# Reordering the start of a perceiver layer: the first pair of x loaded and normalised alone, a fold in two blocks, a query between scores, and ranks in two fp32r matmuls

## The reference

```python
x = x + xattn(layernorm(x), ctx)      # softmax((x Wq + bq)(ctx Wk + bk)^T / 16) (ctx Wv + bv) Wo + bo
x = x + attn(layernorm(x))            # causal, one head of 256
h = layernorm(x)
raw = h @ centroids.T                 # 8 experts
top_idx = top_k(sigmoid(raw + routing_bias), 2)
x = x + shared(h) + sum over the 2 chosen experts of gate * (gelu(h @ Wfc_e) @ Wproj_e)   # width 1024
```

## Time and profile before

| | |
|---|---|
| median of 3 timed runs | 253.61 us (253.21 to 254.71) |
| profiled execution, its own time | 252.07 us |
| its span, first to last instruction | 250.3 us |
| outside the span | 1.77 us |
| TensorE matmul busy | 97% of the span |
| VectorE, ScalarE, GpSimd busy | 61%, 55%, 20% |
| mean rate of all transfers | 296 GB/s |

### The profile page before, as it was taken

How to read it: one execution, slowest core, us unless ns; L and a number is a source line. 1 busy time by engine, 2 the same in 40 slices (tenths; PEclk the granted TensorE clock), 3 DMA queues, 4 the chain that set the end, 5 groups by cost and what they waited for, 6 DMA issues and landing times.

```text
span 250.3 us, 5122 instructions
## 1 busy us (share of the span) xinstructions
PE 242.9 (97%) x1908; PEld 209.6 (84%) x1908; DVE 152.4 (61%) x365; ACT 137.2 (55%) x271; POOL 50.6 (20%) x81
## 2 busy tenths in 40 slices
PE   7999999999999999999998999999999999999994
PEld 6857646366467599999998899999999999999994
DVE  1722246545635788788759147666766766667683
ACT  0725206052152688796776166666666666666641
POOL 5100000000100010420686002102122222226700
PEclk9999999999999999999999999999999999999999
DMA  7999999999999999930166358999989999920132
GB/s 249 425 432 402 417 415 427 384 405 429 351 376 385 352 347 429 427 143 0 67 187 261 101 152 283 373 356 369 370 346 358 363 360 364 335 107 21 56 135 84
DMA packets 13870, 74.12 MB, mean 296 GB/s; under 512 B 1524, under 2 KB 8444, under 8 KB 9500
## 3 DMA queue, kind: packets, MB, share of 16 engines
q1 hardware_dynamic: 12700, 70.59, 74.4%
q0 software_dynamic: 1008, 2.76, 2.9%
q10 hardware_dynamic: 144, 0.53, 0.6%
HBM read 67.56 MB, written 6.32 MB: 295 GB/s over the span
## 4 chain that ended last, share of the span: by engine, by line
PE 72%; DMA 15%; POOL 3%; DVE 3%; ACT 3%; issue 2%; SPq 1%; POOLq 0%; DVEq 0%; ACTq 0%
PE psum L512 64%; DMA raw<-experts_dram 9%; PE psum L760 4%; POOL slot_x_dram L479 3%; DMA slot_x_dram<-second,rows_of 3%; DMA squares<-squares_dram 2%; PE psum L601 1%; PE psum L778 1%; DMA xrow<-slot_x_dram 1%; ACT prob L885 1%; PE psum L821 1%; DVE xn L1046 1%; PE psum L552 0%; PE psum L650 0%; PE psum L692 0%
## 5 line engine op out<-in xcount | busy, mean ns | idle before, releaser
L512 PE MATMUL psum<-xrowT,ring 128*128 128x128 f32 x480 | 58.3, 275 | 0.0
L512 PEld LDWEIGHTS psum<-xrowT,ring 128*128 128x128 f32 x480 | 56.2, 192 | 0.0
L1301 DVE TENSOR_TENSOR dlo<-ring,dhi 128x1024 fp32r<-128x1024 f32 x30 | 38.4, 1281 | 3.7 <-ACT dhi L968 3.7
L1320 DVE TENSOR_TENSOR slot_hlo<-slot_h,slot_hhi 128x512 fp32r<-128x512 f32 x30 | 20.8, 692 | 30.0 <-ACT slot_hhi L996 30.0
L994 ACT ACTIVATE slot_h<-psum 128x512 f32<-128x512 f32 x30 | 18.0, 600 | 35.7 <-PE psum L512 35.7
L512 PE MATMUL psum<-dhi,slot_hhi 128*128 128x256 f32 x120 | 36.3, 302 | 0.1
L512 PE MATMUL psum<-dhi,slot_hlo 128*128 128x256 f32 x120 | 33.8, 282 | 0.0
L512 PE MATMUL psum<-dlo,slot_hhi 128*128 128x256 f32 x120 | 33.8, 282 | 0.0
L968 ACT ACTIVATE dhi<-ring 128x1024 fp32r<-128x1024 f32 x30 | 31.1, 1040 | 0.0
L504 POOL DMA_INDIRECT results_dram<-y_rows,result_row x13 | 15.6, 1199 | 71.8 <-DMA results_dram<-y_rows,result_row 55.3
L512 PE MATMUL psum<-xh,parted 128*128 128x256 f32 x128 | 26.8, 286 | 0.1
(11 more groups left out here) (195 smaller groups left out, 408.2 us busy)
## 6 DMA issues: line engine op xcount, KB each, us to landing
ring<-experts_dram SPq DMA_DIRECT2D x15, 2048.0 KB, 8.2
ctx<-ctx_dram SPq DMA_DIRECT2D x4, 3072.0 KB, 24.5
ctxT_start<-ctxT_start_dram SPq DMA_DIRECT2D x4, 2048.0 KB, 19.0
ctxT_rest<-ctxT_rest_dram SPq DMA_DIRECT2D x4, 1154.0 KB, 21.8
raw<-experts_dram SPq DMA_DIRECT2D x2, 2048.0 KB, 16.4
slot_x_dram<-empty_row SPq DMA_DIRECT2D x1, 1935.0 KB, 16.9
xrow<-slot_x_dram SPq DMA_DIRECT2D x15, 129.0 KB, 7.1
squares<-squares_dram SPq DMA_DIRECT2D x1, 1285.0 KB, 14.2
```

Source lines behind the costliest of these rows:

```text
L512: return pe.matmul(out, lhsT, rhs, start=first, stop=last)
L1301: dve.tensor_tensor(dlo[b % 2][:, steps, :], ring[b][:, steps, C * P:STEP_W], dhi[b % 2][:, steps, :].bitcast(F32), ALU.subtract).then_inc ...
L1320: dve.tensor_tensor(slot_hlo[:, half, :], slot_h[:, half, :], slot_hhi[:, half, :].bitcast(F32), ALU.subtract).then_inc(slot_hlo_ready, 1)
```

## The change

Transfers: pair 0 of x is loaded alone, then squares 0 and 1 in two pieces (one for each half k of the contraction, 1028 contiguous bytes each), then pairs 1 to 3 of x, all on SyncE's queue. cols goes to ScalarE's queue.

Start: VectorE computes the statistics of pair 0 and normalises it before it waits for the rest of x. GpSimd computes rstd of pair 0 between two of its constants, the others after all of them. TensorE folds k = 0 for both halves of the output when its piece is there, then k = 1; transposes and queries pair 0 alone, then pairs 1 and 2 together, and pair 3's query stands between score chunks 1 and 2. ScalarE loads its table early with a copy of one element, copies pair 0 before the broadcasts, and makes two of the three broadcasts later. vecs gets its own bank (2) and is made before wrow.

Ranks: chosen, before, tri and a second matrix of ones are fp32r. before gets a fifth column group in place of total, and ranks are two matmuls, of 40 and 32 columns.

```diff
@@ -118,7 +118,8 @@
         neghalf = sb("neghalf", [P, T])
-        tri = sb("tri", [P, P])
+        tri = sb("tri", [P, P], F32R)
+        ones_r = sb("ones_r", [P, P], F32R)
         ones = sb("ones", [P, P])
@@ -147,6 +148,7 @@
         lsum2 = sb("lsum2", [P, 2])
+        first_of_table = sb("first_of_table", [P, 1])
@@ -155,9 +157,8 @@
         gat = sb("gat", [P, TOP, T, ROUTED])
-        chosen = sb("chosen", [P, T, ROUTED])
-        before = sb("before", [P, T, ROUTED])
-        total = sb("total", [P, ROUTED])
+        chosen = sb("chosen", [P, T, ROUTED], F32R)
+        before = sb("before", [P, T + 1, ROUTED], F32R)
         rank = sb("rank", [P, T, ROUTED])
@@ -259,8 +260,10 @@
-        x_in, query_squares_in, squares_in, cols_in, rows_in = (
-            sem("x_in"), sem("query_squares_in"), sem("squares_in"), sem("cols_in"), sem("rows_in"))
+        x_start_in, x_rest_in, squares_in, cols_in, rows_in = (
+            sem("x_start_in"), sem("x_rest_in"), sem("squares_in"), sem("cols_in"), sem("rows_in"))
+        query_squares_in = [sem("query_squares0_in"), sem("query_squares1_in")]
+        vec_ps, vecs_ready = sem("vec_ps"), sem("vecs_ready")
         ctx_in, ctx_rest_in = [sem("ctx0_in"), sem("ctx1_in")], [sem("ctx0_rest_in"), sem("ctx1_rest_in")]
@@ -314,7 +317,7 @@
-        NORMS = {item: 2 + n for n, item in enumerate(item for item in ORDER if item[0] in ("proj", "z"))}
+        NORMS = {item: 3 + n for n, item in enumerate(item for item in ORDER if item[0] in ("proj", "z"))}
@@ -327,8 +330,10 @@
         def _(sp):
-            sp.dma_start(xs[:, :, :], x_d).then_inc(x_in, 16)
-            sp.dma_start(cols[:, :, :], cols_d.rearrange("(c p) n -> p c n", p=P)).then_inc(cols_in, 16)
+            sp.dma_start(xs[:, 0:1, :], x_d[:, 0:1]).then_inc(x_start_in, 16)
+            for c in range(C):
+                sp.dma_start(squares[:, 0:2, c, :], squares_d[:, 0:2, c, :]).then_inc(query_squares_in[c], 16)
+            sp.dma_start(xs[:, 1:T, :], x_d[:, 1:T]).then_inc(x_rest_in, 16)
@@ -430,13 +435,15 @@
             pool.wait_ge(consts, 4)
-            link(pool.memset(tri[:, :], 1.0))
-            pool.affine_select(out=tri[:, :], in_=tri[:, :], compare_op=ALU.is_ge, fill=0.0, base=-1,
+            pool.tensor_copy(ones_r[:, :], ones[:, :])
+            pool.affine_select(out=tri[:, :], in_=ones[:, :], compare_op=ALU.is_ge, fill=0.0, base=-1,
                                pattern=[[1, P]], channel_multiplier=-1).then_inc(consts, 1)
...
             pool.wait_ge(consts, 6)
+            pool.wait_ge(var_ready, 1)
+            pool.tensor_tensor(rstd[:, 0:1], veps[:, 0:1], neghalf[:, 0:1], ALU.pow).then_inc(rstd_ready, 1)
             link(pool.iota(iota128[:, :], pattern=[[P, ROUTED]], base=0, channel_multiplier=0,
@@ -446,14 +453,14 @@
                            allow_small_or_imprecise_dtypes=True))
-            link(pool.memset(before[:, 0, :], 0.0))
+            link(pool.tensor_copy(before[:, 0, :], empty_row[:, 0:ROUTED]))
             link(pool.memset(ones8[:, :], 1.0))
...
             pool.wait_ge(consts, 7)
-            pool.wait_ge(var_ready, 1)
-            pool.tensor_tensor(rstd[:, :], veps[:, :], neghalf[:, :], ALU.pow).then_inc(rstd_ready, 1)
+            pool.wait_ge(var_ready, 2)
+            pool.tensor_tensor(rstd[:, 1:T], veps[:, 1:T], neghalf[:, 1:T], ALU.pow).then_inc(rstd_ready, 1)
             for what, *args in ORDER:
@@ -511,14 +518,6 @@
-            def fold(b, left, right):
-                for m in range(C):
-                    for k in range(C):
-                        ins = mm(bank(b, m * D, D), squares[:, left, k, m * P:(m + 1) * P],
-                                 squares[:, right, k, 0:D], k == 0, k == C - 1)
-                ins.then_inc(fold_ps, 1)
             def fold_vec(b, at, left, col):
@@ -538,37 +537,50 @@
-            pe.wait_ge(query_squares_in, 16)
-            fold(0, XWQT, XWKT)
+            for k in range(C):
+                pe.wait_ge(query_squares_in[k], 16)
+                for m in range(C):
+                    ins = pe.matmul(bank(0, m * D, D), squares[:, XWQT, k, m * P:(m + 1) * P], squares[:, XWKT, k, 0:D],
+                                    start=k == 0 and m == 0, stop=k == C - 1, skip_group_check=True)
+            ins.then_inc(fold_ps, 1)
+            def transpose_x(t, b, at):
+                pe.wait_ge(xn1_ready, t + 1)
+                for c in range(C):
+                    ins = pe.transpose(bank(b, at + c * P, P), xn[:, t, c * P:(c + 1) * P], ident[:, :])
+                return ins
+            def query(t, b, at):
+                for m in range(C):
+                    for k in range(C):
+                        ins = mm(bank(b, at + m * P, P), aq[:, k, m * P:(m + 1) * P],
+                                 xT[:, k, t * P:(t + 1) * P], k == 0, k == C - 1)
+                return ins
+            pe.wait_ge(consts, 2)
+            transpose_x(0, PT, 0).then_inc(xT_ps, 1)
             pe.wait_ge(cols_in, 16)
-            fold_vec(1, D + 1, XWKT, XBQ)
+            fold_vec(2, 0, XWKT, XBQ).then_inc(vec_ps, 1)
             pe.wait_ge(bcast_ready, 1)
             fold_row(1, 0, XWQT).then_inc(fold_ps, 1)
-            pe.wait_ge(consts, 7)
-            for t in range(T):
-                pe.wait_ge(xn1_ready, t + 1)
-                for c in range(C):
-                    ins = pe.transpose(bank(PT + t // 2, (t % 2) * D + c * P, P),
-                                       xn[:, t, c * P:(c + 1) * P], ident[:, :])
-                if t % 2 == 1:
-                    ins.then_inc(xT_ps, 1)
             pe.wait_ge(fold_act, 1)
-            for t in range(T):
-                pe.wait_ge(xT_sb, t // 2 + 1)
-                tok = slice(t * P, (t + 1) * P)
-                for m in range(C):
-                    for k in range(C):
-                        ins = mm(bank(PO + t // 2, (t % 2) * D + m * P, P), aq[:, k, m * P:(m + 1) * P],
-                                 xT[:, k, tok], k == 0, k == C - 1)
-                if t % 2 == 1:
-                    ins.then_inc(q_ps, 1)
+            pe.wait_ge(xT_sb, 1)
+            query(0, PO, 0).then_inc(q_ps, 1)
+            transpose_x(1, PT + 1, 0)
+            transpose_x(2, PT + 1, D).then_inc(xT_ps, 1)
+            transpose_x(3, CHAIN, 0).then_inc(xT_ps, 1)
+            pe.wait_ge(xT_sb, 2)
+            query(1, PT, 0)
+            query(2, PT, D).then_inc(q_ps, 1)
+            def last_query():
+                pe.wait_ge(xT_sb, 3)
+                query(3, CHAIN, 0).then_inc(q_ps, 1)
             def scores(t, ch):
-                if t % 2 == 0 and ch == 0:
-                    pe.wait_ge(q_sb, t // 2 + 1)
-                if t == 0 and ch == 0:
-                    pe.wait_ge(fold_act, 1)
+                if ch == 0:
+                    pe.wait_ge(q_sb, (1, 2, 2, 3)[t])
+                if t == 0 and ch == 1:
                     pe.wait_ge(fold_dve, 1)
@@ -692,10 +704,14 @@
-            for ch in range(SCH):
+            for ch in range(2):
                 scores(0, ch)
+            last_query()
+            for ch in range(2, SCH):
+                scores(0, ch)
             pe.wait_ge(squares_in, 16)
+            pe.wait_ge(q_sb, 2)
             for m in range(C):
@@ -706,7 +722,6 @@
             ins.then_inc(fold_ps, 1)
-            pe.wait_ge(q_sb, 2)
             pe.wait_ge(bcast_ready, 2)
@@ -714,6 +729,7 @@
             def bias_folds():
+                pe.wait_ge(q_sb, 3)
                 fold_vec(CHAIN, D + 1, AWK, ABQ)
@@ -729,11 +745,10 @@
                 pe.wait_ge(chosen_ready, 1)
+                mm(bank(RANK_BANK, 0, (T + 1) * ROUTED), ones_r[:, :], before[:, :, :].rearrange("p t e -> p (t e)"),
+                   True, False)
                 mm(bank(RANK_BANK, 0, T * ROUTED), tri[:, :], chosen[:, :, :].rearrange("p t e -> p (t e)"),
-                   True, False)
-                mm(bank(RANK_BANK, 0, T * ROUTED), ones[:, :], before[:, :, :].rearrange("p t e -> p (t e)"),
-                   False, True)
-                mm(bank(RANK_BANK, T * ROUTED, ROUTED), ones[:, :], total[:, :], True, True).then_inc(rank_ps, 1)
+                   False, True).then_inc(rank_ps, 1)
@@ -855,30 +870,46 @@
-            act.dma_start(squares[:, 0:2], squares_d[:, 0:2]).then_inc(query_squares_in, 16)
-            act.wait_ge(consts, 7)
-            act.wait_ge(cols_in, 16)
-            for n, col in enumerate((XBK, XBV, ABK)):
+            act.dma_start(cols[:, :, :], cols_d.rearrange("(c p) n -> p c n", p=P)).then_inc(cols_in, 16)
+            act.wait_ge(warm_ready, 1)
+            act.activation(first_of_table[:, :], sm[:, 0:1], ACT.Copy)
+            def spread(n, col):
                 for c in range(C):
...
+            def xT_copy(n, start, stop, b):
+                act.wait_ge(xT_ps, n + 1)
+                act.activation(xT[:, :, start * P:stop * P].rearrange("p c (t n) -> p t c n", n=P),
```

(72 more changed lines are left out.)

## The result

The changed kernel took 255.89 us as a median of 8 runs (254.50 to 256.75), the kernel before 254.04 us beside it (253.21 to 254.99). The ratio is 1.0077, with a 95% interval of 1.0050 to 1.0105: slower by 0.8%. The prediction, 253.5 us with a range of 252.3 to 254.6, was wrong in its time and on the wrong side. The ratios are taken over the fast runs alone, which leaves out 3 of the 11 runs of e5 and 5 of the 12 of e14; medians and ranges are of all runs.

The account below looks back on a forecast made before the run. Up to 84 us the full transfer stream, beside a full TensorE, was taken to set the landings. 0 (start) + 0.1 (stream) - 0.2 (ranks) = -0.1 us on 253.61 gave a median of 253.5 us, range 252.3 to 254.6.

Parts of the forecast that it names:

- the new wait for ctxT_start 1: Sign: TensorE newly waits for this transfer at about 30.5 us; with ctx's wait at 50.7, as long as the start's gain.
- Ranks: Two single-pass matmuls replace three two-pass ones; the scatter starts 0.2 us earlier (0 to 0.4), and this reaches the end.
- Start on TensorE: Up to the second matrix's fold at 20.43 us: 0.7 us gained (-0.8 to +1.5), worth 0 at the end.
- a cap: Landings at 30.5, 50.7 and 81.9 us are set by the stream, limiting an earlier start's gain to TensorE's slack there.
- R3: Rival: the start's small steps make TensorE 0.8 us late at the second fold; 253.9 us, chance 10%.
- Stream: Same bytes, moved by three terms; +0.1 us at raw 0 and at 83.94 us, bounds -0.4 and +1.2.
- Term (a): Squares 0 and 1 and pair 0 of x in pieces of about 1 KB, at 356 against 418 GB/s: +0.3 us.
- (c): Slow first 6 us: cols' small rows now travel beside pair 0, filling idle engine time; -0.4 to 0, taken as -0.2.
- Term (b): SyncE issues ctxT_start 0 behind five transfers, some 0.9 us later; costs up to 0.9 us, taken as 0.
- R2: Rival: engines run dry between 1.6 and 4 us, landings move by 0.9 and 0.3 us; 254.6 us, chance 10%.
- R4: Rival: pair 0 of x doesn't land earlier, so the start stays; the forecast's time, 65% together with the forecast.
- R1: Rival: the waits at 30.5, 50.7 and 81.9 us move with TensorE; 252.7 us, at most 251.7, chance 15%.

Follow-up runs that it names:

- e5: Kernel before with the change's transfers, but squares 0 and 1 in one transfer of whole rows on SyncE's queue; 254.91 us, ratio 1.0079.
- e14: Kernel before with split 15 moved behind feature 21; 257.87 us, ratio 1.0103.
- e1: Kernel before with four one-element copies put ahead of ScalarE's program; 252.38 us, ratio 0.9958.
- e7: Kernel before with the load of ring buffer 1 issued behind the wait for the scatters and the row loads; 253.41 us, ratio 0.9993.
- e9: Kernel before with sixteen short instructions ahead of ScalarE's program; 254.1 us, ratio 1.0000.
- e13: Kernel before with split 15 moved to right behind split 14; 252.44 us, ratio 0.9971.
- e2: Kernel before with only the change's ranks (two fp32r matmuls); 253.97 us, ratio 0.9996.
- e11: Kernel before with the change's ranks and four short instructions ahead of ScalarE's program; 254.03 us, ratio 0.9999.
- e4: Changed kernel with squares 0 and 1 back on ScalarE's queue in one transfer of whole rows, cols on SyncE's; 254.3 us, ratio 1.0023.
- e8: Changed kernel with e4's squares and cols, and e7's later load of ring buffer 1; 253.15 us, ratio 1.0006.
- e15: Changed kernel with e4's squares and cols, and split 15 right behind split 14 as in e13; 254.74 us, ratio 1.0036.
- e10: Changed kernel with sixteen short instructions near the start of ScalarE's program; 255.54 us, ratio 1.0068.
- e12: Changed kernel unchanged, run again in a second session; 255.41 us, ratio 1.0069.
- e3: Kernel before with only the change's transfers, its compute waiting for all of them; 4 runs, 253.4 us without the clock's fall, 255.85, 257.73 and 257.79 with it.
- e6: Kernel before with squares 0 and 1 in two transfers of 1028-byte pieces, both on ScalarE's queue; 256.56 us, ratio 1.0161.

## Why the prediction was wrong, step by step

The profiles add up in a simple way, which the prediction could have used. From the first slot's transpose to the end there are 110.4 to 110.5 us in every kernel. Ahead of it stand three stretches: up to norm2's transpose on TensorE, from there to the first scatter, and from there to the first slot. All in us:

| kernel | raw 0 parted | norm2 on TensorE | to the first scatter | to the first slot |
|---|---|---|---|---|
| before | 81.88 | 83.94 | 35.94 | 19.91 |
| e1, e7, e9, e13, e14 (order and ranks of before) | 81.30 to 82.08 | 83.50 to 84.14 | 35.92 to 35.98 | 19.87, 22.26, 22.38, 20.18, 22.56 |
| e2, e11 (ranks new) | 81.90, 81.35 | 83.96, 83.46 | 35.60, 35.64 | 22.20, 22.34 |
| e4, e8, e15 (order and ranks new, squares whole) | 81.99, 81.78, 81.96 | 84.33, 84.15, 84.37 | 35.68, 35.68, 35.62 | 22.26, 22.26, 19.87 |
| after, e10, e12 (all new) | 83.17, 82.68, 82.30 | 85.63, 84.78, 84.54 | 35.61, 35.62, 35.63 | 22.44, 22.44, 21.02 |

For the two profiled executions: 1.69 us at norm2, -0.33 for the ranks and 2.53 behind the scatter make 3.9, the difference of their spans to 0.1.

Against the forecast of 253.5 us the changed kernel is 2.4 us slow. Of these 0.4 are the base: the kernel before, taken beside it, stood at 254.04 and not at 253.61 us. The rest is a difference of +1.85 us where -0.1 was forecast. The prediction had named its own sign of failure, a raw 0 off by over 0.5 us, and it came: 83.17 against 81.88 us. The fold before 5.4 us came too (5.10), and the new wait for ctxT_start 1, but at 32.3 and not at 30.5 us.

*Ranks: right, and a little small.* The prediction took -0.2 us (0 to 0.4). The stretch from norm2 to the scatter is shorter by 0.24 to 0.38 us in all eight profiles with the new ranks, about 0.3.

*Start on TensorE: wrong in sign.* The prediction took 0.7 us of gain at the second fold and gave it no worth, since a cap holds behind it. The second fold is at 20.73 to 21.39 us with the new start, against 20.27 to 20.54. It failed in two steps. The gain was read from the squares' landing, up to 1.57 us, while the fold also stands behind 20 warm-up matmuls that end at 5.3 to 5.7 us: about the 0.74 us of idle of the earlier trace rows was to be had. And the small waits were given as a bound of -0.8 and then outweighed; they cost 0.87 - 0.13 = 0.7 us of idle between 8 and 20 us (e4). That is R3. It reaches norm2: the three kernels with the new start and whole squares have it at 84.28 us in the mean, the six of the first two rows of the table at 83.78, so 0.5 us, as R3 had said.

*Stream: the term was mis-sized. This is the step that failed.* The prediction took +0.1 us at raw 0 (-0.4 to +1.2). The changed kernel's three profiles (after, e10, e12) have raw 0 at 82.72 us in the mean, the eight with the transfers of before at 81.62 (81.30 to 82.08): +1.1 us. The bytes of the first 8 us, summed over the four slices, group in the same way: 2258 to 2376 KB in those eight, 2162 to 2246 with x in two parts and the squares whole (e4, e5, e8, e15), 1818 to 2046 with the pieces on SyncE's queue (after, e3, e10, e12). Most of the lateness comes with the last step, the pieces: with x in two parts alone raw 0 stands at 81.31 to 81.99 us, not clear of the spread of before.

Term (a) priced the pieces at 356 against 418 GB/s from a stretch of 1 KB rows, which makes 1.48 us of the 514 KB of squares. That row was of another kind: rows that start on a 1 KB raster, at the end of the kernel. The packets' own records in the traces give what x and the squares took of the 16 engines' time: 3.5 to 3.9 us (3.7 in the mean) in the four kernels with the pieces on SyncE's queue, 3.0 to 3.5 (3.3) in the other thirteen, e6 among them with 3.3. That is 0.4 us more. It lies in the pieces (1.85 to 1.94 us, against 1.73 as whole rows on the same queue in e5 and 1.54 as pieces on ScalarE's queue in e6) and in the rest of x behind them (1.20 to 1.56 us against 0.97 to 1.10 in e4, e5, e8 and e15). So the price of (a), 0.3 us, was near, and the sum was too small by what stands in no term of it: the other 0.7 of the 1.1 us. The -0.2 us of (c) didn't come either: the first slice moved 12 GB/s against 18, the second 241 against 258. What the 0.7 us are made of stays open; the runs show only that they come with the pieces at the head of SyncE's queue (after, e3, e10, e12) and not with the same pieces on the other queue (e6).

Term (b), the issues behind each other, falls by the same records. (It counted five transfers ahead of ctxT_start 0 on SyncE's queue; there are four, and in the kernel before two.) That transfer is issued at 2.70 us instead of 1.68, but its first packet starts at 5.2 us in both kernels, behind those of x, while the first packet of x starts 1.0 us after its issue. So it waited for the engines, and not for its issue. R2 came true in its size and not in its mechanism: ctx 1 at 52.75 us and raw 0 at 83.17 are near its 51.9 and 83.0, but the engines didn't run dry. They were 0.93 to 0.96 busy in each slice from 2 to 8 us.

Raw 0 is one of two limits at norm2. In before the transpose follows the start of the parting by 2.06 us, with 0.28 us of idle; in the changed kernel's three profiles it follows by 2.46, 2.10 and 2.24 us, without idle. So TensorE, late from the second fold and from ctxT_start 1, gets there about as late as the stream does. The two losses meet at norm2 and don't add: 84.98 us in the mean against 83.78, +1.2.

On the pieces the Trainium skill ("DMA: Bandwidth & Descriptors", "How a descriptor splits into AXI transactions") has a row that doesn't start on a 256-byte boundary fetch the bytes before it as well; worked out for rows of 1028 bytes that is up to a fifth more, an estimate. The direction agrees with the runs. The size of the loss doesn't: by the packets' records the pieces took 1.85 to 1.94 us against 1.73 of whole rows on the same queue, within that estimate, but the slice fell from 452 to 276 GB/s, by over a third. No run here parts the row's size from where it starts.

*The rivals.* The change does what it says (pair 0 of x lands 2.3 us after its issue, the fold starts at 5.10 us), so R4 falls. R1's opposite happened: TensorE meets the caps later, with 0.39 us of idle at 32.31 and 0.40 at 52.75 us. R2 and R3, 10% each, both came true in size, and at once, a case that the prediction didn't have. Added up, 1.2 and 0.5 us less the ranks' 0.2 would have been 255.1 us, nearer to the result, but by luck: at norm2 they overlap, and 1.2 us is all that arrives there.

*The tail: the step that isn't in the prediction.* It said that from the scatter to 139.79 us only GpSimd and the transfers count. That was read from one execution, which had no halt. In 43% of before's timed runs there is a fall of the clock behind it. The halt with the fall lengthens the stretch from the scatter to the first slot by 2.3 to 2.7 us in profiles, without the fall (e12) by 1.1. The changed kernel showed the fall in 13 of 19 runs. Whether the change makes it likelier isn't settled: with the sixteen pads it was 8 of 12, and e4, e8 and e15, which differ from it in the squares and one more edit at most, had 17 of 34 together. The median of before itself, 253.61 us of three runs (253.21 to 254.71), may already have had some of this in it, and with runs in two groups 1.5 us apart a median jumps with the share of each. The prediction took that median as its base and made its range of the rivals' times, with nothing for it.

*What stays open.* At like clock the medians are 1.4 us apart. The profiles give 1.2 at norm2 (84.98 in the mean of three, 83.78 in that of six) less 0.3 for the ranks, so 0.9. The other 0.5 us lies in runs that no trace shows; by e12 against the first profile, a stream that is slower in some runs than in others is a candidate, and only argued. The cause of ScalarE's idle time before feature 21 is open: not its instruction count, not the ring load, not split 15. Counted from 0.90 us after TensorE's first matmul for that product, the part without a reason is nothing in before, 0.9 to 2.3 us in e1, e5, e6, e13, e14 and e15, and 3.7 to 4.0 us in the other ten. An obvious rival, that ScalarE waits for its own code to be loaded, has nothing for it in the traces: no packet of the two instruction queues starts within this idle time in any of the seventeen profiles (in the changed kernel the nearest start at 123.8 and 140.7 us). Other ways to wait that leave no packet aren't excluded.

## What to carry to other kernels

Before a transfer at the head of a saturated stream is cut into shorter rows, compare the GB/s of its first microseconds slice by slice: shares of 0.93 to 0.96 went with 241 to 380 GB/s here, and what the changed kernel lost there was still missing 75 us later. An earlier start of one stage is worth no more than the idle time that TensorE shows before it, and each new hand-over between engines that the reordering brings has to be paid out of that. Look at several runs and their granted clocks before trusting one profile's tail: here two groups of runs lie 1.5 us apart, more than the effect that was forecast.

## What the runs showed of the hardware that was not expected

- ScalarE stands idle before one and the same instruction longer than its input explains in sixteen of the seventeen profiles. Ten show 4.7 to 4.8 us of idle, with a releaser that the trace can't name; before, the seventeenth, shows 1.11 us, all of it waiting for TensorE.
- TensorE's granted clock fell to its lower level for 3.4 us after idle stretches of 2.0 to 2.4 us that end between 131 and 134 us in ten profiles, for 6.8 us after one of 2.25 us at 8 us in e6, and stayed at 1.00 after one of 2.22 us in e12.
- The slice from 4 to 6 us, in which rows of 1028 bytes cut out of rows of 4112 travel on SyncE's queue, has 267 to 283 GB/s in three profiles and 388 in a fourth, against 377 to 480 with whole rows. On ScalarE's queue (e6) it has 399, but there the fold that waits for the pieces started 2 us later, beside the large rows of the other queue.
